# ScalarE issues the DMAs that spread the first three batches' queries, with the first loads and the order of work on all engines rewritten, in a two-layer transformer kernel on one core

## The reference

```
x = x + _L0_xattn_ref(_layernorm(x), ctx, ctx, mask, Wq, bq, Wk, bk, Wv, bv, Wo, bo)   # 16 heads of 8, causal, bf16 projections
x = x + _L0_ffn_ref(_layernorm(x), Ws1, Ws2, W1, W2, Wr)                               # shared MLP and 8 small experts
x = x + _L1_xattn_ref(_layernorm(x), ctx, bias, wq, wk, wv, wo)                        # 16 heads of 8, f32, additive bias
x = x + _L1_ffn_ref(_layernorm(x), q_w, k_w, v_w, o_w, sel_v_w, sel_o_w, route_scale)  # SwitchHead: 8 heads, 8 experts each
```

## Time and profile before

| | us |
|---|---|
| median of 3 runs | 1430.54 |
| lowest, highest | 1429.03, 1432.64 |
| the profiled execution's own time | 1428.65 |
| its span, first to last instruction | 1426.9 |
| TensorE busy | 1362.8 (96%) |
| VectorE busy | 1284.9 (90%) |
| ScalarE busy | 1219.8 (85%) |
| GpSimd busy | 921.2 (65%) |
| chain that ended last | TensorE 87%, VectorE 4%, GpSimd 3% |

### The profile page before, as it was taken

How to read it: one execution, slowest core, us unless ns; L and a number is a source line. 1 busy time by engine, 2 the same in 40 slices (tenths; PEclk the granted TensorE clock), 3 DMA queues, 4 the chain that set the end, 5 groups by cost and what they waited for, 6 DMA issues and landing times.

```text
span 1426.9 us, 34376 instructions
## 1 busy us (share of the span) xinstructions
PE 1362.8 (96%) x9585; PEld 923.6 (65%) x9585; DVE 1284.9 (90%) x5266; ACT 1219.8 (85%) x4234; POOL 921.2 (65%) x1409
## 2 busy tenths in 40 slices
PE   3578999999999999999999999999999999999997
PEld 2355666666666666666667666666666666666654
DVE  3768999999999999999999999999999999999986
ACT  3567888999888899988888998888899888889886
POOL 3123666676676667666666776667667666766777
PEclk7579999999999999999999999999999999999999
DMA  4530001000111100011110001111000111100000
GB/s 126 155 93 26 27 28 29 15 18 28 29 30 30 29 17 18 26 29 30 29 30 21 16 25 29 29 30 30 23 16 24 28 30 29 30 20 11 22 3 5
DMA packets 99967, 44.97 MB, mean 32 GB/s; under 512 B 21249, under 2 KB 99777, under 8 KB 99777
## 3 DMA queue, kind: packets, MB, share of 16 engines
q1 hardware_dynamic: 82560, 34.13, 8.6%
q10 hardware_dynamic: 17216, 8.65, 2.1%
HBM read 25.70 MB, written 8.52 MB: 24 GB/s over the span
## 4 chain that ended last, share of the span: by engine, by line
PE 87%; DVE 4%; POOL 3%; issue 2%; SPq 2%; ACT 1%; DMA 1%; POOLq 0%; ACTq 0%; DVEq 0%
PE psC L327 58%; PE psA L327 13%; PE psB L327 6%; PE psB L555 4%; PE psC L637 2%; SPq L3800 2%; DVE PTB L2366 1%; POOL accO L3413 1%; PE psA L489 1%; POOL TE L3401 1%; DVE nmA L2241 1%; DVE TE L2499 1%; POOL v_sb L3406 1%; PE psA L442 1%; PE psB L576 1%
## 5 line engine op out<-in xcount | busy, mean ns | idle before, releaser
L1341 ACT ACTIVATE TE<-psC,gateO 128x128 f32<-128x128 f32 x1024 | 290.0, 379 | 30.1 <-PE psC L327 27.0
L2499 DVE SCALAR_TENSOR_TENSOR TE<-psC,gateO,TE 128x128 f32<-128x128 f32 x1024 | 286.9, 342 | 21.7 <-PE psC L327 11.6
L1341 ACT ACTIVATE TE<-psC,gate 128x128 f32<-128x128 f32 x1024 | 299.2, 402 | 6.8 <-PE psC L327 1.9
L2499 DVE SCALAR_TENSOR_TENSOR TE<-psC,gate,TE 128x128 f32<-128x128 f32 x1024 | 284.1, 340 | 7.4 <-PE psC L327 3.0
L3413 POOL TENSOR_TENSOR accO<-accO,TE 128x512 f32<-128x512 f32 x192 | 247.0, 1286 | 53.9 <-DVE TE L2499 44.7
L327 PE MATMUL psC<-Oh,ch 128*128 128x512 f32 x512 | 269.0, 525 | 0.0
L327 PE MATMUL psC<-Vh,xTh 128*128 128x512 f32 x512 | 263.1, 514 | 0.7 <-ACT PS L1341 0.7
L3401 POOL TENSOR_TENSOR TE<-TE 128x256 f32<-128x256 f32 x256 | 189.8, 741 | 56.4 <-DVE TE L2499 41.4
L327 PE MATMUL psC<-Oh,cl 128*128 128x512 f32 x512 | 202.1, 395 | 0.0
L327 PE MATMUL psC<-Vh,xTl 128*128 128x512 f32 x512 | 201.6, 394 | 0.0
L327 PE MATMUL psC<-Vl,xTb 128*128 128x512 bf16 x512 | 199.7, 390 | 0.0
(11 more groups left out here) (231 smaller groups left out, 3391.0 us busy)
## 6 DMA issues: line engine op xcount, KB each, us to landing
bdB<-k_rows SPq DMA_DIRECT2D x128, 64.0 KB, 2.3
k_rows<-Kc SPq DMA_DIRECT2D x96, 64.0 KB, 2.0
Qs<-Qc SPq DMA_DIRECT2D x96, 64.0 KB, 1.9
raw<-in_L_ffn_v_w ACTq DMA_DIRECT2D x8, 512.0 KB, 4.0
raw<-in_L_ffn_o_w ACTq DMA_DIRECT2D x8, 512.0 KB, 3.9
x_sb<-in_x SPq DMA_DIRECT2D x32, 64.0 KB, 2.1
ctx_sb<-in_ctx SPq DMA_DIRECT2D x32, 64.0 KB, 2.0
Qb<-Qc SPq DMA_DIRECT2D x128, 8.0 KB
```

Of the source, the lines that this page charges most:

```text
L1341: return A.activation(o, i, func, **kw)
L2499: m = V.scalar_tensor_tensor(TE[:, i, e], psC[:, p, e * P:(e + 1) * P], gates[:, e:e + 1], TE[:, i, e], ALU.mult, ALU.add)
```

## The change

Three things change. First, for batches 0, 1 and 2 ScalarE issues the four query DMAs (`a_spread`), with the same waits, and SyncE's `a_queries` skips these batches. Second, `inputs(0)` becomes SyncE's first work, the selector weights come after the other small weights, and `q_w` before `k_w`; ahead of `inputs(1)` stands also `bias(0)`. Third, the lists of all five engines are written in another order: much in `start()`, some neighbours in `period(i)` and `end()`. No computation is added or removed.

```diff
+        EARLY = 3
...
@@ -1434,6 +1433,14 @@
+            def a_spread(b):
+                act.wait_ge(s_zero, 4)
+                act.wait_ge(a_qs, b + 1)
+                act.wait_ge(a_s, 4 * b)
+                act.wait_ge(a_q2, b)
+                for j in range(NJ):
+                    A.dma_start(Qb[SLOT * j + ROW0:SLOT * j + ROW0 + HD], Qc0[SLOT * j:SLOT * (j + 1)]).then_inc(s_qA, 16)
+
...
@@ -1634,16 +1641,17 @@
                 a_xt(0)
+                a_queries(0)
+                a_spread(0)
+                products()
                 b_keys(0)
-                a_queries(0)
-                products()
                 cut(0)
...
@@ -3870,7 +3880,7 @@
             def a_queries(b):
-                if b not in BATCHES:
+                if b not in BATCHES or b < EARLY:
                     return
...
@@ -3934,96 +3944,95 @@
             def start():
+                inputs(0)
                 values0()
                 out0()
+                loads1()
                 weights_switch()
-                loads1()
-                inputs(0)
                 keys0()
                 queries0()
+                products()
+                products2()
                 masks(0)
-                products2()
-                products()
+                bias(0)
                 inputs(1)
-                a_queries(0)
                 a_keys(0)
                 a_masks(0)
...
```

More of the change, by code:

```diff
@@ L691, in start @@
                 a_scores(0, 3)
+                b_keys(0)
                 a_maxt(0)
@@ L743, in start @@
                 a_queries(2)
+                b_keys(1)
+                b_proj(0)
                 a_x1t(1)
@@ L920, in start @@
                 values(1, 5, 0)
+                b_keys(4)
                 a_values(5)
@@ L923, in start @@
                 a_xt(5)
-                b_keys(4)
                 values(1, 6, 1)
@@ L1006, in start @@
                 values(2, 6, 0)
+                b_keys(5)
                 values(2, 7, 1)
                 a_queries(6)
-                b_keys(5)
                 values(2, 7, 0)
@@ L1667, in start @@
                 a_gap(0)
+                cut(5)
                 a_shared(0, 0)
-                cut(5)
                 a_shared(0, 1)
@@ L1799, in start @@
                 a_shared(3, 1)
+                b_keys(3)
                 c_context(0, 1)
@@ L2523, in start @@
                 a_stats(0, 2)
-                a_norm(0)
-                keys0()
-                queries0()
+                ones()
                 operand_q()
-                b_keys(0)
                 hidden_keys()
                 operand_k()
+                keys0()
+                a_norm(0)
+                queries0()
                 pads()
+                a_stats(1, 0)
+                a_stats(1, 1)
+                a_stats(1, 2)
                 selectors()
-                a_stats(1, 0)
                 a_max(0, 0)
@@ L2584, in start @@
                 b_bias(0, 2)
+                cut(9)
                 b_bias(0, 3)
-                cut(9)
                 a_withmax(1)
-                a_norm(2)
                 cut(10)
                 cut(11)
+                a_attend(1, 0)
+                a_attend(1, 1)
                 b_attend(0, 0)
                 b_attend(0, 1)
-                a_attend(1, 0)
-                a_attend(1, 1)
                 cut(12)
+                b_third(0)
                 a_first(1, 0)
-                b_third(0)
+                c_stats(0, 0)
                 a_first(1, 1)
                 a_stats2(1, 0)
-                c_stats(0, 0)
                 a_stats2(1, 1)
                 a_stats2(1, 2)
+                c_stats(0, 1)
+                c_stats(0, 2)
                 a_norm2(1)
                 cut(13)
-                b_keys(1)
                 a_top(1, 0)
@@ L2608, in start @@
                 a_top(1, 2)
-                c_stats(0, 1)
+                b_keys(1)
                 a_routed(1, 0)
@@ L2919, in start @@
                 a_norm2(5)
-                c_stats(4, 1)
+                b_third(4)
                 values(2, 7)
-                b_keys(5)
-                c_stats(4, 2)
+                c_share(3, 1)
+                c_stats(4, 0)
                 a_top(5, 0)
```

928 lines of the change are left out of this document (460 added, 468 removed).

## The result

| | before | after |
|---|---|---|
| median of 6 runs each, us | 1429.01 | 1421.77 |
| lowest, highest | 1427.34, 1432.64 | 1420.45, 1422.74 |
| profiled execution, own time | 1428.65 | 1422.74 |
| its span | 1426.9 | 1421.0 |

The ratio is 0.9942, with a 95% interval from 0.9928 to 0.9957: the change is faster by 0.58%. The forecast was 1427.5 us, 0.2% less and within what can be told from no change; the range from 1421 to 1433 holds the result, the forecast itself is wrong by 5.7 us. The profiled execution is the slowest of the six.

The account below looks back on a forecast made before the run. TensorE bounds the full period, so only an earlier start could win: 3.5 us at 130 us less 0.5 in the periods gave 3.0, hence 1425.65, plus 1.89 to the median: 1427.5 us, range 1421 to 1433.

Parts of the forecast that it names:

- First scores: Batch 0's start: with the queries off SyncE's queue the mask row leaves earlier, scores 5.3 us earlier (4.1 to 5.9).
- The second weight load: ScalarE's load of `cut(1)` goes out later, near 21 us, behind `b_keys(0)`: 0.7 us lost (0 to 1.5).
- `xTA` of batches 0 and 1: Four issues on ScalarE delay the copy making `xTA`: 1.9 us lost for batch 0, 2.4 for batch 1.
- more of the gain lasts: Rival, chance 0.36: a faster clock at the start, or ScalarE's issues falling into waits; 1420 to 1426 us, likeliest 1424.
- the clock: Within that rival: denser early work keeps the upper clock level from 80 to 90 us, batch 1's feed-forward up to 3 us faster.
- Strand b: Its first scores, at 61.88 us, gain 3 us (2 to 4), since a 1.28 us cut now precedes its root.
- Batch 2 and 130 us: Earlier `a_withmax` (0.9 us) and SwitchHead normalisation (0.6) join about 2 us left: 3.5 us (0 to 7) earlier at 130 us.
- Period: One more variance ahead of `a_withmax` costs 0.02 us in each of 25 periods: 0.5 us lost (0 to 2.5).
- End: The last batches' lists are nearly the same: 0 us.
- Hidden by the cuts: Rival, chance 0.15 with the shared queue: the sixteen cuts' load waits tie batches 0 to 3, hiding the start's gain; 1430 us.
- A beat missed on VectorE: Rival, chance 0.12: one more wait ahead of `a_withmax`, or a late bias row, returns in 25 periods; 1435.5 us.
- The shared descriptor generator: Rival, counted within hidden's 0.15: ScalarE's and SyncE's issues can't run together, mask row 2.8 us later than forecast; 1429 us.

Follow-up runs that it names:

- after_again: The changed kernel once more, unchanged, for a second profile and more times; 1421.38 us, ratio 0.9941.
- scalar_only: The kernel before with only the query DMAs of batches 0 to 2 issued by ScalarE, at the changed kernel's places; 1430.08 us, ratio 1.0005.
- before_again: The kernel before once more, unchanged, for a second profile; 1428.94 us, ratio 0.9997.
- new_end: The kernel before with the changed kernel's end part alone, from batch 31's second scores on, SyncE's list kept; 1431.17 us, ratio 0.9994.
- new_period: The kernel before's start part, up to around batch 6, then the changed kernel's period and end; 1428.37 us, ratio 0.9989.
- new_start: The changed kernel's start part, up to batch 6, then the period and end of the kernel before; 1424.11 us, ratio 0.9958.
- spread_behind: The changed kernel with ScalarE's query DMAs of batches 1 and 2 put behind the copy that makes `xTA`; 1422.86 us, ratio 0.9954.

## Why the prediction was wrong

The direction and the mechanism at the first scores were right. The sum was too small by several terms. Of the 5.7 us, 1.5 are the base: the forecast stood on a median of 1430.54 by three runs, which is 1429.01 by six. The other 4.2 are the gain, 7.2 in place of 3.0.

**First scores.** Forecast 5.3 us earlier (4.1 to 5.9), issue of the mask row near 14.7. Measured 6.1, with the issue at 15.21 and the scores at 17.21, just below the 17.4 that I had as the least (`M` started 0.16 earlier). The landing, 1.87 us, was at the better end of my estimate (2 to 4.5). This was the largest term, and it was right within 0.8.

**The second weight load.** Forecast 0.7 lost. It went out at 20.14 (near 21 was said), and `UA`, the copy behind the exponentials, came 6.04 us earlier (34.70 to 28.66): nothing was lost. So 6.0 us of lead stood where I had 4.6. It was luck that 4.6 was nearly right at the transpose (4.8, and 5.6 in the second pair of profiles): the wait for batch 2's input, which I had not booked, took the rest.

**`xTA` of batches 0 and 1: the step that failed.** I let the four issues begin when the cut's two casts had ended and so booked 1.9 and 2.4 us. The distance from the transpose to `xTA` grew by 1.2 us for batch 0 (0.79 to 1.99; to 1.31 in after_again) and by 0.1 for batch 1 (0.51 to 0.63). Two things were missed. ScalarE's queue issues its next DMA while a cast before it still runs (37.46, inside the casts from 37.05 to 38.20). The trace of the kernel before had it: the load that stands behind the copy of `M` in ScalarE's list goes out while that copy runs.

```profile
17.88 1.02 ACT L1341 ACTIVATE M<-psC 128x1024 f32<-128x1024 f32 x1 [5.65 <-PE psC L327]
17.90 0.57 ACTq L1376 DMA_DIRECT2D raw<-in_L_ffn_v_w  x1
```

And the new order has the queries ready early, so at 76.65 the four issues fill a wait for TensorE that was there anyway. The order comparison had the second in it: `a_queries(1)` stands ahead of `a_x1t(0)` on TensorE. scalar_only shows what I should have costed as a case of its own: without that order it is 3.5 and 3.8 us, more than I booked, and the whole gain. So the distinction was missing: how early the queries are ready. The two losses of 4.3 us were 1.3, but not all of that reached the sum: the lead at the transpose of batch 1 was 3.3 us and not 4, so at `xTA` it was 3.2 (3.7 in the second pair) where I had "about 2" (and 4 - 2.4 is 1.6). The rival "more of the gain lasts" named this cause ("the issues fall into waits"), and it is the case that came. Its other cause, the clock, did not show: from 80 to 90 us it was 0.60 and 0.83 in the kernel before, 0.50 and 0.75 in the changed one.

**Strand b.** Forecast 3 us earlier for its first scores (2 to 4). Measured 5.5. `x2` itself came 4.9 us earlier (51.95 to 47.06) and not 3.3; of these 1.6 us the step above made 0.7, and 0.7 came between `xTA` and `x2`, which drew nearer by 1.3 us where I had booked 0.6 for the moved `cut(5)`. The cut between its statistics and the root cost 0.3 us, not 1.3: from `x2` to b's transpose it took 3.14 us, against 2.87. From that transpose to b's scores it took 6.18 against 7.06. b's third query DMA went out 2.87 us behind the transpose and not 3.65. SyncE's queue was empty both times; b's queries themselves came earlier, 0.5 us of it because ScalarE copied `xTB` 0.38 us behind the transpose and not 0.87, where a cut had held it.

**Batch 2 and 130 us.** Forecast 3.5 (0 to 7). `a_withmax` of batch 2 ran at 94.95 in place of 99.81, 4.9 earlier where b's transpose had gained 3.4, so 1.4 us were won on the way, where I had booked half of 1.8 for the swap. At ctx 4 the gain is 4.6 in the first pair of profiles and 6.9 in the second. "TensorE is full from about 126 us" holds by the windows.

**Period.** Forecast 0.5 lost. The matmul ahead of the second scores is followed after 0.42 us, as before:

```profile
752.66 0.39 PE L328 MATMUL psC<-Vl,xTb 128*128 128x512 bf16 x1
753.08 0.29 PE L328 MATMUL psA<-Q,bdA 128*128 128x128 bf16 x2
```

The undisturbed period is 41.38 us in both kernels. The one more variance fitted into the gap. The 23 periods from ctx 7 to ctx 30 still took 0.7 us less: 953.3 us by the mean of nine profiles with the old period (952.0 to 953.9) and 952.6 by seven with the new one (951.8 to 953.2). A likely reason, not tried by itself, is strand b's third query DMA: in the undisturbed periods it has 0.2 to 1.0 us to spare in the kernel before and 0.9 to 1.0 in the changed one.

**End.** Forecast 0, measured 1.3 us. I called the lists "nearly the same" and did not look for waits there, though the old end had several of 0.2 to 0.5 us. This term and the period's were together 2.5 us too low. The start was too low by 1.0 by the two pairs of profiles (4.5 at ctx 7 where 3.5 were booked at 130 us), and by more if more profiles are taken, as the next paragraph shows.

Sum by the means of two profiles: 4.5 + 0.7 + 1.3 = 6.5 us, where 3.0 was forecast. The medians say 7.2 and the ratio 8.3, because the kernel before spreads upwards: its 12 runs of before_again lie between 1427.3 and 1432.7, those of the changed kernel between 1419.5 and 1422.7. More profiles show where: new_end and new_period start as the kernel before does, new_start as the changed one. At ctx 7 the four with the old start stand at 268.65, 269.11, 269.94 and 273.83 us, the three with the new one at 265.32, 263.39 and 262.44. That is 6.7 us by the means and not 4.5, and with 0.7 and 1.3 it makes 8.7, near the ratio's 8.3.

**The rivals.** "Hidden by the cuts" did not come: the cuts moved with the chain (41.80 to 37.05, 81.17 to 76.69). "A beat missed on VectorE" did not come either. The shared descriptor generator is worth a word. ScalarE's four issues took 3.58 us and SyncE's four, at the same time, 3.09; alone, both on SyncE, the same two groups took 3.09 and 2.81, and four on ScalarE alone took 2.84 (scalar_only). Side by side they are a tenth to a quarter slower, and together they took 3.6 us (11.74 to 15.32) where one behind the other needs 5.9. The Trainium skill, "Perfetto Trace Analysis", "DMA Instruction — HWDGE", says that one generator serves the sequencers and is locked for the use of one. By that, the mask row would have gone out 2.8 us later. The trace bears out a small part of it. The Trainium skill says in "DMA: Bandwidth & Descriptors", "Issuing engines are not separate DMA queues", that only the sequencer's time is saved. This does not hold as a bound here: 3.6 us of issuing were saved and the landing came 6.2 earlier, since the mask row also got ahead of two large loads.

## What to carry to other kernels

When DMA issues move to a compute engine's queue, cost them twice: at the place where their data are ready, and at the place where the next instruction of that engine is wanted; they are free only if the first lies well ahead of the second, and put behind the second they may stand in front of a third (spread_behind). Moving the producer of the data ahead of the other branch decided between nothing gained and 2.4 us, so an issue and the order of its producer are one edit. The first mask row or other small DMA on which a chain waits should leave ahead of the large loads. In the nine profiles in which it left before ScalarE's first load of 512 KB it landed in 1.7 to 1.9 us, in the one in which it left behind one such load in 3.45, and in the six in which it left behind two in 4.4 to 5.0.

## What the runs showed of the hardware

**The clock at the start differs between executions of the same instructions.** The kernel before and new_period have the same lists up to batch 6 and stand at 82.23 and 82.21 us at the transpose of batch 1. From 90 to 100 us the granted clock was then 0.89 in the one and 0.55 in the other, between the levels of 2.4 and 1.2 GHz, and at the same transpose of batch 2 they stand at 113.19 and 115.80: 2.6 us for nothing in the program. Two more profiles have this start: new_end, with 0.53 in that window, and before_again, with 1.00. From the one transpose to the other the two with the low clock took 33.6 and 33.0 us, the two others 31.0 and 30.8. The window of before, then of new_period:

```profile
90.00:100.00 10.00, 7.10 (x41) 4.56 (x40) 8.20 (x36) 4.84 (x15) 1.70 (x3) 0.89 0.19 54
```

```profile
90.00:100.00 10.00, 7.95 (x33) 6.08 (x34) 6.10 (x17) 2.52 (x8) 1.70 (x3) 0.55 0.19 54
```

The changed kernel and new_start differ likewise. They stand at 78.89 and 78.88 us, with TensorE busy 4.60 and 4.61 of the 10 us before 80; then the clock from 80 to 90 was 0.50, the lower level, and 0.79, and batch 2's transpose came at 108.82 and 107.00. So a single profile tells a start's gain to about 2 us only. How much of the spread of the runs this makes is not shown, and the mean clock of a run doesn't order the times: of before_again's runs one of 1427.32 us had 0.976, one of 1432.69 us 0.990 and one of 1432.70 us 0.971. The recorded clock can also miss a slow stretch. From 20 to 80 us it says 0.54 for the kernel before and 1.00 for new_period, but the first scores' matmul of 512 columns took 0.58 us in both, and 0.38 in after_again.

**Some DMAs land late in the same batches every time.** Strand b's third query DMA lands 1.9 us after its issue and then has 0.95 us to spare. In batches 8, 21 and 24 it took 2.5 to 3.1 us in both kernels and in both profiles of each, and the period grew by up to 0.6 us; in batch 14 it did so for the changed kernel only. The landings of the three query DMAs of batch 21 in the kernel before, behind them the same one batch earlier:

```profile
DMA to landing us min/median/max: 1.9/2.0/3.1
```

```profile
DMA to landing us min/median/max: 1.9/1.9/1.9
```

The profile has a likely cause. Beside the program's DMAs it lists packets of the kind "instruction", of 8 or 16 KB; I take them for the loading of the program's instructions. Of strand b's 1104 query DMAs of batches 8 to 30 in all 16 profiles, 812 had no such packet in flight, and none of them took over 2.3 us to land. Of the 292 that had one, 115 did, up to 3.7 us. The queues while the late DMA of batch 21 was in flight (before, 911.2 to 913.8 us), then one batch earlier (869.0 to 872.2):

```profile
q1 hardware_dynamic: 288, 0.13, 17.5%
q8 instruction: 1, 0.02, 2.5%
```

```profile
q1 hardware_dynamic: 441, 0.20, 21.0%
```

The instruction loads stand at places of the program, which fits that the same batches are late every time. That they are the cause was not tried by moving one, and why some of the DMAs beside them land on time is open.
